# A graph layer and a mixture of experts in one kernel: eight blocks instead of six go through every expert where they lie

## The reference, cut to what matters

```python
x = x + _L0_gnn_ref(_layernorm(x, axis=-1), W_self, W_neigh, b, src, dst)
# of the second half, on the normalised x:
logits = jnp.einsum('bsd,de->bse', xn, Wr) + br
top_vals, top_idx = jax.lax.top_k(logits, K)              # K = 2 of E = 8
w_full = ...                                              # softmax of the two, 0 for the other six
for e in range(E):
    h = jax.nn.gelu(xn @ W1[e] + b1[e])                   # 256 -> 512
    y = y + (h @ W2[e] + b2[e]) * w_full[..., e, None]    # 512 -> 256
```

## Time and profile of the kernel before

| | |
|---|---|
| median of 3 runs | 1274.3 us (1267.23 to 1276.89) |
| profiled execution | 1265.94 us |
| its span in the trace | 1263.9 us |
| granted TensorE clock over the span | 0.969 of full |
| PE busy / weight loads | 1091.7 us (86%) / 969.2 us (77%) |
| DVE busy | 867.7 us (69%) |
| ACT busy | 435.7 us (34%) |
| POOL busy | 941.4 us (74%) in 980 instructions |

### The profile page before, as it was taken

How to read it: one execution, slowest core, us unless ns; L and a number is a source line. 1 busy time by engine, 2 the same in 40 slices (tenths; PEclk the granted TensorE clock), 3 DMA queues, 4 the chain that set the end, 5 groups by cost and what they waited for, 6 DMA issues and landing times.

```text
span 1263.9 us, 22166 instructions
## 1 busy us (share of the span) xinstructions
PE 1091.7 (86%) x6356; PEld 969.2 (77%) x6357; DVE 867.7 (69%) x2812; ACT 435.7 (34%) x811; POOL 941.4 (74%) x980
## 2 busy tenths in 40 slices
PE   0379998989987989999989898986898887988987
PEld 0258887979876878998878787876787776977877
DVE  8876667677677666777876676854677764655447
ACT  6822333223334333434433433432324321311131
POOL 7567777777767777777777777777777777777775
PEclk9989999999999999999998999999999998999999
DMA  9989998866647476666765657656587669776777
GB/s 350 331 260 351 342 311 268 290 194 212 190 136 225 147 228 206 223 202 201 218 196 184 197 187 210 181 165 208 170 274 221 212 209 262 227 232 200 228 218 236
DMA packets 163993, 287.57 MB, mean 228 GB/s; under 512 B 25632, under 2 KB 93344, under 8 KB 163744
## 3 DMA queue, kind: packets, MB, share of 16 engines
q1 hardware_dynamic: 115280, 153.36, 37.0%
q0 software_dynamic: 45696, 124.88, 33.0%
q10 hardware_dynamic: 2896, 7.87, 1.7%
HBM read 228.81 MB, written 57.20 MB: 226 GB/s over the span
## 4 chain that ended last, share of the span: by engine, by line
PE 67%; DVE 13%; issue 7%; DMA 4%; POOL 4%; ACT 2%; SPq 1%; DVEq 1%; POOLq 0%; ACTq 0%
PE bank L961 22%; PE bank L1037 17%; PE bank L1063 10%; PE bank L1071 6%; PE bank L949 3%; PE bank L990 3%; PE bank L992 3%; POOL ring L688 2%; ACT heap L798 2%; PE bank L1087 1%; DVE heap L1467 1%; DVE agg L1310 1%; PE bank L1098 1%; DMA expert_out<-inside 1%; PE bank L1007 1%
## 5 line engine op out<-in xcount | busy, mean ns | idle before, releaser
L688 POOL DMA_INDIRECT ring<-feature_table,src_sb x756 | 740.0, 979 | 251.3 <-issue 229.0
L961 PE MATMUL bank<-ring,onehot 128*128 128x257 f32 x1544 | 388.5, 396 | 99.0 <-issue 51.0
L961 PEld LDWEIGHTS bank<-ring,onehot 128*128 128x128 f32 x1544 | 299.1, 197 | 155.7 <-issue 103.7
L863 ACT ACTIVATE heap<-heap 128x512 f32<-128x512 f32 x139 | 87.6, 630 | 331.9 <-DVE heap L1467 331.9
L1467 DVE TENSOR_TENSOR heap<-bank,b_sb 128x512 f32<-128x512 f32 x139 | 95.8, 689 | 148.6 <-PE bank L1037 79.9
L1063 PE MATMUL bank<-heap 128*128 x728 | 182.6, 395 | 12.3 <-DVE y_out L1476 6.8
L1037 PE MATMUL bank<-row_t,heap 128*128 128x128 f32 x1456 | 180.4, 278 | 0.6 <-DVE heap L1467 0.6
L1037 PEld LDWEIGHTS bank<-row_t,heap 128*128 128x128 f32 x1456 | 174.6, 195 | 2.3 <-issue 0.8
L1063 PEld LDWEIGHTS bank<-heap 128*128 128x128 f32 x728 | 137.6, 197 | 30.6 <-issue 13.3
L1310 DVE SCALAR_TENSOR_TENSOR agg<-bank,in_first,agg 128x257 f32 x196 | 94.3, 481 | 95.3 <-PE bank L961 51.3
L1271 DVE TENSOR_TENSOR onehot<-iota,target 128x512 f32<-128x512 f32 x196 | 134.4, 686 | 7.3 <-DVE xf L1327 5.3
(11 more groups left out here) (193 smaller groups left out, 1253.1 us busy)
## 6 DMA issues: line engine op xcount, KB each, us to landing
heap<-in_w SPq DMA_DIRECT2D x139, 512.0 KB
expert_out<-empty_row SPq DMA_DIRECT2D x68, 256.0 KB
ring<-feature_table,src_sb POOLq DMA_INDIRECT x756
row<-expert_rows SPq DMA_DIRECT2D x91, 128.5 KB, 4.4
xf<-in_x SPq DMA_DIRECT2D x49, 128.0 KB
ff<-feature_table SPq DMA_DIRECT2D x49, 128.0 KB
expert_out<-inside SPq DMA_DIRECT2D x46, 128.0 KB
expert_out<-y_out SPq DMA_DIRECT2D x45, 128.0 KB
```

The source lines that it names most:

```text
L688: pool.indirect_dma_start(group_row(t, i)[:, 0:D], None, x if t < RAW else table, bass.IndirectOffsetOnAxis(src_sb[:, k:k + 1], 0)).then_i ...
L863: act.activation(hid[s], hid[s], ACT.Gelu).then_inc(S.gelu, 1)
L961: last = pe.matmul(bank[t % 2][:, 0:D + 1], onehot[:, q, i, :], group_row(t, i), start=(i == 0), stop=(i == GT - 1))
```

## The change

The list of blocks that go through all experts in place gets three blocks for one: the 16th, 22nd and 28th to be finished (numbers 15, 21, 27) replace the 19th (number 18). Eight blocks instead of six are dense, and block 18 becomes a routed one.

```diff
-DENSE_BLOCKS = (0, 3, 6, 9, 18, 47)
+DENSE_BLOCKS = (0, 3, 6, 9, 15, 21, 27, 47)
```

## The result

| | before | after |
|---|---|---|
| median of 4 runs each, side by side | 1271.5 us (1267.2 to 1276.9) | 1291.9 us (1290.5 to 1293.1) |
| profiled execution, span | 1265.94, 1263.9 us | 1290.54, 1288.8 us |
| PE busy, weight loads | 86%, 77% | 88%, 78% |
| POOL busy, instructions | 74%, 980 | 73%, 972 |

The changed kernel takes 1.0166 times as long, 95% interval 1.0128 to 1.0204. That is 20 us more by the medians and 24.6 by the profiled executions; 13 were forecast, and 1291.9 lies inside the range.

The account below looks back on a forecast made before the run. POOL was taken to bound, PE close behind: 19.8 us of holds, less 5.3, plus 5.1, less 6.5, made +13 us on the profiled 1265.94; with 8.4 us up to the runs' median, 1287.5 us, range 1267 to 1303.

Parts of the forecast that it names:

- the ring: POOL's gathers wait for PE four groups behind: gather 127 may not start before group 123 is summed, at 769.0 us.
- the holds: POOL's waits for PE's groups, from about slot 90 up to gather 127: 19.8 us lost in small pieces.
- PE's work in slots 63 to 123: Work at the full clock, summed from prices between starts of weight loads: 367.6 us.
- 1.045: PE's breaks in slots 63 to 123: time over work, taken from busy stretches before, making 384.1 us of 367.6.
- so the fuller PE gets both amounts back: Slots 63 to 119: PE, having fewer breaks, returns to clock 1.00 and regains 5.0 and 6.7 us.
- Edits taken as nothing: Extra matrix loads, DVE's work for ten more units and added waits, slots 63 to 119: no time of their own.
- The 1.08: Upper end for PE's breaks in slots 63 to 123, twice the nearest stretch's: POOL loses 32.7 us.
- What POOL sheds: Four scatters fewer ahead of gather 127, 5.3 us, and two merges fewer in the loop, 5.1 us: together 10.4 us.
- The end: Slots 180 to 195: four merges, 10.0 us, gone from POOL; PE can use only 6.5 us of it.
- The first, PE takes it up: Rival: PE absorbs the added work in slots 63 to 119, POOL never held; 1264 to 1268 us, chance 0.13.
- The second: Rival: the shared result bank doubles PE's breaks to 1.08, 32.7 us lost instead of 19.8; 1300 us, chance 0.17.
- The third, PE bounds throughout: Rival: PE bounds from end to end, so all added PE work counts, 40 us; 1314 us, chance 0.03.

Follow-up runs that it names:

- half the hidden values: Changed kernel, the 24 dense units of blocks 15, 21 and 27 multiplying only 256 of 512 hidden values: 1263.9 us, 0.9943 of the kernel before.
- PE's work added: Kernel before, with the hidden products of 26 tiles in slots 63 to 119 done twice: 1284.9 us, 1.0130 of the kernel before.
- both edits: Changed kernel, DVE's weighted sums ahead of list making and early tile lists made in two halves in following slots: 1269.8 us, 0.9992 of the kernel before.
- the sums placed first: DVE's weighted sums ahead of list making: on the changed kernel 1278.2 us (1.0064), on the kernel before 1263.7 us (0.9935).
- Halves alone: Changed kernel, each early list of tiles made by DVE in two halves in following slots, sums left in place: 1285.8 us, 1.0120 of the kernel before.

## Why the prediction was right, and which of its terms were off

**The mechanism** was right: POOL bounds before, the change loads PE in slots 63 to 123, the ring carries PE's lateness to POOL, the holds cease at gather 127, and the end is later by what is left of it. The runs with half the hidden values and with PE's work added show each side of it alone. The places were not as forecast: the holds were to come "in small pieces from about slot 90 on", between 560 and 780 us; the first is at 458.25, and two make 10.6 of the 28.3 us.

| step | predicted | measured |
|---|---|---|
| PE's work in slots 63 to 123, full clock | 367.6 us | 370.3 us (busy time with both edits, clock 1.00) |
| time over work there | 1.045 | 395.6 / 370.3 = 1.068 |
| of it, time over busy time | 1.045 | 395.6 / 376.9 = 1.050 |
| of it, busy time added by a lower clock | 0 | 376.9 - 370.3 = 6.6 us |
| slots 63 to 119 | 361 us | 367.9 us |
| group 123 ends | 769.0 us | 787.0 us |
| holds behind gather 64 | 19.8 us | 28.3 us |
| slots 180 to 195 | 85.5 us | 82.4 us |
| profiled execution | 1279 us (1265.94 + 13) | 1290.54 us |
| median | 1287.5 us | 1291.9 us |

**PE's work** was priced to within 1%: in sum, the prices from start to start of weight loads carry over.

**The clock is the term that was most mis-sized.** The stretch was 11.5 us longer than the forecast 384.1. Of these 2.7 are work (370.3 against 367.6) and 2.2 are idle time (18.7 against the 16.5 that 1.045 leaves). The other 6.6 are the same 2284 instructions at a lower clock. The step that failed is thus "so the fuller PE gets both amounts back": PE was fuller, 95% busy, and its granted clock in the stretch was still 0.98; it came to 1.00 when the long breaks were gone. The ratio 1.045, read as time over busy time, was nearly right at 1.050; over work at the full clock, as the sum uses it, it is 1.068.

Behind the breaks, and so behind the clock, stands the step in "Edits taken as nothing": "A dense unit costs DVE about as much as a tile (three instructions each), so ten more units on 98.0 of 133.5 us leave room." DVE's busy share is indeed no higher (278.4 of 395.6 us, 70%); its order is what counts, 5 us in one piece ahead of the sums. The 1.08 at the range's other end covered the sum of both.

**Group 123 at 787.0** is 18 us late, not 11.5: 6.5 of it stood at slot 62 already. Up to there the kernels differ only in the preparation of block 15, yet group 62 ended at 384.9 and 385.6 us in the two profiles without block 15 in the list, and between 387.1 and 391.4 in the four with it (DVE's order as it was in all six). Part of that is the spread of executions, and a few us may be the change's; no run separated the two. With the sums placed first it ends at 378.6 us without the change and 379.4 with it.

**What POOL sheds** came as counted: 80 scatters in place of 84, all merges done by slot 179. **The end** gave more back than forecast, 9.6 us in place of 6.5: PE ran slots 180 to 195 at 1.00 with 81.24 of 82.40 us busy, without the breaks allowed for. By the spans, 24.9 us apart, the account is the forecast 13, 11.5 from the stretch and 6.5 ahead of it, less 3.1 in slots 180 to 195, which makes 27.9. The 3.0 us over were won back in two places: slot 180 starts 35.1 us later than before (1156.1 against 1121.0), where 19.6 + 18.0 = 37.6 would follow, and the part behind the last group is 0.6 us shorter (1288.8 - 1238.5 against 1263.9 - 1213.0). What shortened them was not traced.

**What was luck.** The sum missed the profiled execution by 11.6 us and put the growth at about half of what it was. The median came out within 4.4 us because the forecast added 8.4 us, by which the profiled execution of before lay under the median of its first three runs. After the change that distance is 1.4 us, so 7 of the 11.6 us cancelled. No term of the sum accounts for that.

**The rivals.** The first, PE takes it up, fell with the 28.3 us of holds. The second named the result bank, at 1.08 and 1300 us, a little above the 1.068 and 1291.9 measured; but its evidence was the wrong row: line 1071's waits for line 1502 are 8.6 us after the change as before it. They lie in the first dense blocks, and the sums placed first took them away (with them line 1071 waits for line 1502 for 1.4 us in all). In part it was right all the same: what grew are waits for this bank by one kind of unit for the other, line 1071 for 1476 from 1.5 to 6.6 us and line 1063 for 1502 to 5.1 us, the largest of each (3.74 and 3.82) where DVE was making a list. The third, PE bounds throughout, fell: no hold behind 787.27. The Trainium skill's page "Perfetto Trace Analysis", section "Optimization Strategy", says that the most-contended engine can change from one regime of a kernel to the next. This trace agrees: PE bounds slots 63 to 123 at 95% busy, POOL the slots behind them at an unchanged 0.30 us between gathers.

**Halving.** The Trainium skill's page "Perfetto Trace Analysis", section "Optimizing Scalar/DVE Operations", advises that where VectorE isn't saturated but makes bubbles on another engine, breaking up its instructions may let work finish sooner. Here that held in part, for a chain of small instructions rather than for one. Halves alone left the stretch at 398.0 us; halves with the awaited sums ahead of them brought it to 380.8.

## What to carry to other kernels

Ask of an engine at 70% not only how busy it is but what is its longest uninterrupted piece, and who waits for the instruction behind it: 5 us of bookkeeping, repeated every 12 slots, cost nothing clear of the spread behind gather 64 while POOL set the pace; when PE did, three of five such lists made breaks of 2.1 to 3.8 us, and what was added to any of the five came through whole. Do not give an engine the full clock in a forecast because it will have more to do: here 95% busy with a few long breaks ran at 0.98. When work is moved from a bounding engine to the next one, count the slack of the stretch in which it lands, and move no larger piece at a time than fits there.

## What the runs showed of the hardware that was not expected

A break costs more than its length. Windows of the changed kernel around the break of slot 110: before it, and the eight matmuls behind it.

```profile
688.00:692.50 4.50, 4.50 (x34) 4.18 (x33) 3.43 (x21) 1.91 (x2) 3.04 (x4) 1.00 0.53 175
...
696.46:699.75 3.29, 3.29 (x8) 2.69 (x9) 2.90 (x9) 1.49 (x2) 0.00 (x0) 0.54 0.51 153
```

The granted clock was 1.00 (2.4 GHz) up to the break and 0.54 in the 3.29 us behind 3.74 idle microseconds, so nearly all of it at the lower level of 1.2 GHz. The eight matmuls took 3.45 us; the eight of line 1063 at 777.90, the same product for a tile, took 1.93:

```profile
777.90 1.93 PE L1063 MATMUL bank<-heap 128*128 x8
```

The break's price is thus some 1.5 us above its length, and 6.6 us over the stretch, by the busy times of the same 2284 instructions with and without the long breaks (376.9 and 370.3). The prediction had given PE the full clock back because it had more to do; it had, and lost it again behind the long breaks.
